# One common last slot behind the optional ones, its f32 mixing, and its columns cut as a half and two quarters

## The reference

```
x = x + mix(x, W0[c])                          # 64x64 per batch, across the rows, 16 choices
x = x + mix(x, W1[c])                          # the same c, so one 64x64 matrix does for both
x = x + x @ W2.T + 0.5 * (x @ A[l]) @ B.T      # shared 1024x1024 and a low-rank part, 5 choices
x = x + x @ W3[e].T                            # 1024x1024 per batch, e is one of 8, drawn from 3 to 7
```

## Time and profile before

| what | us |
|---|---|
| median of 3 runs (lowest, highest) | 395.53 (394.69, 395.9) |
| the profiled execution, its own time | 394.66 |
| its span in the profile | 392.9 |
| PE busy | 380.2 (97%) |
| DVE busy | 268.3 (68%) |
| ACT busy | 231.2 (59%) |
| POOL busy | 123.3 (31%) |
| end of the last DVE instruction | 388.18 |

### The profile page before, as it was taken

The page is one execution under the profiler, slowest core; times in us unless marked ns, Lnnn a source line. Parts: engine busy times, 40 slices in busy tenths (PEclk is TensorE's granted clock), DMA queues, the critical chain, the costliest instruction groups (busy, mean ns, idle before and its releaser), DMA issues.

```text
span 392.9 us, 7604 instructions
## 1 busy us (share of the span) xinstructions
PE 380.2 (97%) x1736; PEld 316.4 (81%) x1736; DVE 268.3 (68%) x285; ACT 231.2 (59%) x307; POOL 123.3 (31%) x163
## 2 busy tenths in 40 slices
PE   8999999999999999999999999899999999999990
PEld 8888888888888888888888887688888888888860
DVE  4746967865855958547967439953699546899563
ACT  3798859387232775244483549554677357777361
POOL 0000340100003000024865427763258434576400
PEclk9999999999999999999999999999999999999996
DMA  7984902740348475406526224742276322762223
GB/s 225 396 313 158 375 3 79 261 180 19 107 173 288 182 277 166 180 21 214 175 93 221 58 55 123 260 133 55 56 235 211 97 57 56 270 219 54 56 58 88
DMA packets 24219, 61.37 MB, mean 156 GB/s; under 512 B 1938, under 2 KB 2066, under 8 KB 24146
## 3 DMA queue, kind: packets, MB, share of 16 engines
q1 hardware_dynamic: 23808, 60.30, 46.1%
q10 hardware_dynamic: 338, 0.24, 0.2%
HBM read 52.15 MB, written 8.39 MB: 154 GB/s over the span
## 4 chain that ended last, share of the span: by engine, by line
PE 96%; issue 1%; DVE 1%; ACT 0%; POOL 0%; ACTq 0%; DVEq 0%; POOLq 0%
PE ps L1400 44%; PE ps L1286 13%; PE ps L1287 13%; PE ps L1288 13%; PE ps L1427 4%; PE ps L1313 4%; PE ps L1325 2%; PE ps L1257 1%; PE ps L1265 1%; DVE stage L1236 0%; DVE stage L1177 0%; ACT stage L706 0%; DVE aT L1214 0%; PE ps L1446 0%; ACT stage L798 0%
## 5 line engine op out<-in xcount | busy, mean ns | idle before, releaser
L1400 PE MATMUL ps<-ring,aT 128*128 x784 | 180.8, 389 | 0.0
L1400 PEld LDWEIGHTS ps<-ring,aT 128*128 128x128 f32 x784 | 147.1, 188 | 30.8 <-issue 0.4
L1286 PE MATMUL ps<-ring 128*128 128x512 f32 x224 | 88.3, 394 | 0.0
L1287 PE MATMUL ps<-ring 128*128 128x512 f32 x224 | 88.0, 393 | 0.0
L1288 PE MATMUL ps<-ring 128*128 128x512 f32 x224 | 87.9, 392 | 0.0
L429 POOL TENSOR_TENSOR aT<-xT,aT 128x512 fp32r<-128x512 f32 (+1 forms) x36 | 56.3, 1585 | 51.3 <-ACT aT L685 45.2
L1149 DVE TENSOR_TENSOR ring<-raw,ring 128x1024 f32 (+1 forms) x40 | 63.8, 1655 | 5.1 <-ACT ring L671 5.0
L694 ACT ACTIVATE aT<-ps 64x1024 fp32r<-64x1024 f32 x32 | 32.7, 1021 | 48.1 <-PE ps L1400 47.6
L1177 DVE TENSOR_TENSOR stage<-ps,stage 64x1024 f32<-64x1024 f32 x30 | 36.7, 1222 | 26.3 <-ACT stage L706 25.7
L1166 DVE TENSOR_TENSOR aT<-ps,aT 64x1024 fp32r<-64x1024 f32 x32 | 39.1, 1222 | 22.6 <-ACT aT L694 21.9
L1288 PEld LDWEIGHTS ps<-ring 128*128 128x128 f32 x224 | 42.6, 190 | 9.0
(11 more groups left out here) (82 smaller groups left out, 314.5 us busy)
## 6 DMA issues: line engine op xcount, KB each, us to landing
raw<-w3t SPq DMA_DIRECT2D x40, 512.0 KB, 4.4
ring_f<-xt SPq DMA_DIRECT2D x8, 1024.0 KB, 7.7
raw<-xt SPq DMA_DIRECT2D x8, 1024.0 KB, 5.1
out<-stage SPq DMA_DIRECT2D x30, 256.0 KB, 3.0
ring_f<-wt SPq DMA_DIRECT2D x4, 1024.0 KB, 7.4
xT<-xt SPq DMA_DIRECT2D x3, 1024.0 KB, 9.5
xT<-wt SPq DMA_DIRECT2D x2, 1024.0 KB, 15.2
ring_f<-xt SPq DMA_DIRECT2D x4, 256.0 KB, 6.4
```

What stands on the lines that cost most here:

```text
L1286: pe.matmul(dst, hi_of(qw)[:, k, cs], hi_of(qx)[:, k, :], start=start and k == 0, stop=False, skip_group_check=True)
L1287: pe.matmul(dst, hi_of(qw)[:, k, cs], lo_of(qx)[:, k, :], start=False, stop=False, skip_group_check=True)
L1400: last = pe.matmul(acc(i)[:, n, :], x3_split(i, k, start, P), ring[:, bass.ds(off + (part * D + n * 512), 512)], start=(k == 0 and j == 0) ...
```

## The change

The slots that may be missing now stand in front of one common last slot. With m = n_slots - 1, slots 0 to 14 run always, slots 15 to 18 stand nested in `If(n_slots > i + 1)`, and behind them comes the last slot, whose number m, plan word and semaphore counts are in registers. Since buffers alternate between odd and even slots, it is written twice, in `If(odd < 1)` and `Else`. Each engine reads the last slot's word and that of the slot ahead of it early, in slot 2 (`end_slot`; PE spreads its register work over slots 2, 3 and 4). All slots ahead of the last one have the regular order: 4 tiles, the mixing of slot i-1, 4 tiles.

In the last slot PE does the left 512 columns in 8 tiles, mixes the slot ahead, then does columns 512 to 767 in 8 tiles and columns 768 to 1023 in 6 and 2 tiles, with 256 columns to a matmul. Each part is mixed by a single f32 matmul with a matrix that POOL makes (`mixers_last`): ACT copies 128 rows of the sum to SBUF in f32 (`last_rows`), and no low part is split off. Both halves of the pair or both parts of the single sum are dealt with in this one matmul, so that one copy brings a part to `stage`: DVE copies the first two, ACT the third. Ahead of the last mixing stand 6 matmuls of 256 columns whose result isn't used (`warm(BRIDGE, ...)`). SP stores the first two parts, ACT the third. Stores count on two semaphores, for odd and even slots, in place of one for each slot, and SP waits for two semaphores at the end.

POOL also clears the 128x128 tile `last_mix` once, before slot 0. The core of the diff:

```diff
+LOOK = 2
...
-WARM = 20
+WARM, BRIDGE = 20, 6
...
-MIX_AT = 7
+END_AT = 6
...
+    last_mix = sb("last_mix", [P, P], F32, offset=cells_at)
+    last_row = sb("last_row", [P, D], F32, offset=aT_at + 4 * KT * CT)
...
-    def end_ps(i, h, n):
-        return acc(i - 1)[:, h, :] if n == 0 else mixed_ps[h][:, 1, :]
+    END_COLS = (slice(0, 512), slice(512, 768), slice(768, D))
+    def end_acc(p, part):
+        return (acc(p)[:, 0, :], acc(1 - p)[:, 1, 0:256], acc(p)[:, 1, 256:512])[part]
+    def end_ps(p, part):
+        return (acc(1 - p)[:, 0, :], acc(p)[:, 0, 0:256], acc(1 - p)[:, 1, 0:256])[part]
...
+    def end_slot(eng, n_slots):
+        more = eng.snap(n_slots & (SURE - 1))
+        m = within(eng, more + ENDS, ENDS, SLOTS - 1)
+        word, ahead = (eng.value_load(plan[0:1, bass.ds(m + at, 1)], min_val=0, max_val=2 ** WORD - 1) for at in (HEAD, HEAD - 1))
+        return m, within(eng, ((more + 1) >> 1) + ENDS // 2, ENDS // 2, (SLOTS - 1) // 2), word, ahead
+    def within(eng, value, lo, hi):
+        return nc.s_assert_within(eng.snap(value), lo, hi)
...
+            def last(p):
+                sp.wait_ge(s("end_sum"), 2)
+                store(1 - p, ahead, "end_ahead")
+                store_last(p, end_word)
+            with sp.If(odd < 1):
+                last(0)
+            with sp.Else():
+                last(1)
...
+            def mixers_last(word):
+                cs = [pool.value_load(toks[0:1, 0, bass.ds(b, 1)], min_val=0, max_val=NC_ - 1) for b in batches(word)]
+                def whole(rows, c, cols):
+                    one = as_f32(tab[rows, bass.ds(c, 1), :]).rearrange("p c n -> p (c n)")
+                    return pool.tensor_tensor(last_mix[rows, cols], one[:, 0:T], one[:, T:P], ALU.add)
+                with pool.If(get(word, SINGLE) < 1):
+                    whole(slice(0, P), cs[0], slice(0, T)).then_inc(s("end_st"), 1)
+                    pool.wait_ge(s("end_st"), 1)
+                    pool.memset(last_mix[T:P, 0:T], 0.0).then_inc(s("end_st"), 1)
+                    pool.wait_ge(s("end_st"), 2)
+                    whole(slice(T, P), cs[1], slice(T, P)).then_inc(s("end_st"), 1)
+                with pool.Else():
+                    whole(slice(0, P), cs[0], slice(0, T)).then_inc(s("end_st"), 3)
...
+            for i in range(ENDS):
                 earlier, word = step(i, earlier, word)
+                if i == LOOK:
+                    end_word = end_slot(pool, n_slots)[2]
             with contextlib.ExitStack() as nested:
-                for i in range(SURE, SLOTS):
-                    nested.enter_context(pool.If(n_slots > i))
+                for i in range(ENDS, SLOTS - 1):
+                    nested.enter_context(pool.If(n_slots > i + 1))
                     earlier, word = step(i, earlier, word)
+            mixers_last(end_word)
...
+            def last_rows(p, part):
+                act.wait_ge(s("end_left"), part + 1)
+                act.activation(last_row[:, END_COLS[part]], end_acc(p, part), ACT.Copy).then_inc(s("end_rows"), 1)
+            def last(p):
+                act.wait_ge(s("steps"), end_steps)
+                act.wait_ge(s("mixed"), end_mixed - 1)
+                rows_hi(1 - p)
+                act.wait_ge(s("mixed"), end_mixed)
+                last_rows(p, 0)
+                act.wait_ge(s(f"stored{1 - p}"), end_stored + 32 * (p - 1))
+                mixed_cols(1 - p, ahead)
+                last_rows(p, 1)
+                last_rows(p, 2)
+                act.wait_ge(s(f"stored{p}"), end_stored)
+                act.wait_ge(s("end_mixed"), 3)
+                act.activation(stage[:, p, END_COLS[2]], end_ps(p, 2), ACT.Copy).then_inc(s("end_out2"), 1)
+                act.wait_ge(s("end_out2"), 1)
+                act.dma_start(out_part(end_row, 2), stage[0:T, p, END_COLS[2]]).then_inc(s("end"), 16)
...
+            def last(p):
+                rows_lo(1 - p, two_ahead)
+                mixed_sum(1 - p, ahead, two_ahead, "end_sum")
+                dve.wait_ge(s(f"stored{p}"), end_stored)
+                for part in range(2):
+                    dve.wait_ge(s("end_mixed"), part + 1)
+                    dve.tensor_copy(stage[:, p, END_COLS[part]], end_ps(p, part)).then_inc(s("end_out"), 1)
...
+            def mix_last(p, part):
+                pe.wait_ge(s("end_st"), 3)
+                pe.wait_ge(s("end_rows"), part + 1)
+                pe.matmul(end_ps(p, part), last_mix[:, :], last_row[:, END_COLS[part]], start=True, stop=True)\
+                  .then_inc(s("end_mixed"), 1)
...
+                if i == LOOK:
+                    looked.extend(end_slot(pe, n_slots))
+                elif i == LOOK + 1:
+                    looked.append(record(looked[2]))
+                elif i == LOOK + 2:
+                    m = looked[0]
+                    looked.extend((pe.snap(m & 1), within(pe, m * 2, 2 * ENDS, 2 * SLOTS), within(pe, m * 4, 4 * ENDS, 4 * SLOTS)))
...
+            def end_products(p, passes, part, tiles=(0, KT)):
+                count8, offs, _ = end_record
+                cols = END_COLS[part]
+                for k in range(*tiles):
+                    if part == 0:
+                        pe.wait_ge(s("w_lo"), count8 + (k + 1 + WBASE - KT))
+                    off = offs[k // HALF] + (k % HALF) * UNIT
+                    for j, (start, split) in enumerate(passes):
+                        last = pe.matmul(end_acc(p, part), x3_split(p, k, start, P),
+                                         ring[:, bass.ds(off + (split * D + cols.start), cols.stop - cols.start)],
+                                         start=(k == 0 and j == 0), stop=(k == KT - 1 and j == len(passes) - 1))
+                if tiles[1] == KT:
+                    last.then_inc(s("end_left"), 1)
+            def last_slot(p):
+                def columns(passes):
+                    end_products(p, passes, 0)
+                    pe.wait_ge(s("st"), end_st)
+                    pe.wait_ge(s("r_lo"), end_r_lo)
+                    pe.wait_ge(s("staged"), end_r_lo - 2)
+                    mix(1 - p, get(ahead, SINGLE))
+                    end_products(p, passes, 1)
+                    mix_last(p, 0)
+                    end_products(p, passes, 2, (0, END_AT))
+                    mix_last(p, 1)
+                    end_products(p, passes, 2, (END_AT, KT))
+                pe.wait_ge(s("s_lo"), end_r_lo + 4)
+                pe.wait_ge(s("r_lo"), end_r_lo - 2)
+                with pe.If(end_record[2] < 1):
+                    columns(PAIR)
+                with pe.Else():
+                    columns(ALONE)
+                warm(BRIDGE, acc(1 - p)[:, 1, 256:512])
+                mix_last(p, 2)
...
+            ahead, end_record, odd, end_r_lo, end_st = looked[3:]
             with contextlib.ExitStack() as nested:
-                for i in range(SURE, SLOTS):
-                    with pe.If(n_slots == i):
-                        mix_last(i - 1, earlier[2], 1)
-                    nested.enter_context(pe.If(n_slots > i))
+                for i in range(ENDS, SLOTS - 1):
+                    nested.enter_context(pe.If(n_slots > i + 1))
                     earlier, mine = slot(i, earlier, mine)
-                mix_last(SLOTS - 1, earlier[2], 1)
+            with pe.If(odd < 1):
+                last_slot(0)
+            with pe.Else():
+                last_slot(1)
```

More of the change, by code:

```diff
@@ L464, in _ @@
             pool.wait_ge(s("plan"), 1)
+            pool.memset(last_mix[:, :], 0.0).then_inc(s("zeroed"), 1)
             adapter_eyes(0, 0)
@@ L472, in step @@
             def step(i, earlier, word):
[L473 to L478, removed]
+                following = slot_word(pool, i + 1)
+                slot_lo(i + 1, following)
                 if i == 0:
@@ L753, in step @@
                     adapter_part(i, word, LOAD_B, NEXT_B, (HALF, KT))
[L754 to L757, removed]
+                    act.wait_ge(s("mixed"), i)
+                    if i >= 3:
+                        act.wait_ge(*stored(i - 3))
+                    mixed_cols((i - 1) % 2, earlier)
                 return word, following
[L760 to L781, removed]
-                    second = slice(T // 2, T)
-                    for n in range(2):
-                        act.wait_ge(s("end_staged"), n + 1)
-                        act.dma_start(out_half(rows[0], n, second), stage[second, i % 2, 512 * n:512 * (n + 1)]).then_inc(s("end"), 16)
@@ L804, in _ @@
             with contextlib.ExitStack() as nested:
-                for i in range(SURE, SLOTS):
-                    with act.If(n_slots == i):
-                        last(i - 1, earlier)
-                    nested.enter_context(act.If(n_slots > i))
+                for i in range(ENDS, SLOTS - 1):
+                    nested.enter_context(act.If(n_slots > i + 1))
                     earlier, word = step(i, earlier, word)
-                last(SLOTS - 1, earlier)
+            with act.If(odd < 1):
```

(15 more changed lines are left out.)

253 lines of the change are left out of this document (94 added, 159 removed).

## The result

The changed kernel takes 398.44 us (six runs, 397.29 to 399.16) against 394.66 for the kernel before beside it: a ratio of 1.0091, with a 95% interval from 1.0072 to 1.011. It is slower by 0.9%, some 3.8 us. The profiled execution has a span of 397.2 us, 4.3 more than before. That lies in the wide range of the prediction, 391.8 to 401, and on the side it gave the largest chance, but 2.4 us from its point of 396.0 and outside the 394.6 to 397.5 that it gave the case it chose. The ratios leave out one run of the kernel before, beside e5 to e8, that took 777.88 us.

The account below looks back on a forecast made before the run. PE, busy 380.2 of 392.9 us, was taken as the bound. Tail -4.0, registers +0.3 and jumps +4.2 gave +0.5: span 393.4, median time 396.0 us; 8 in 10 range 391.8 to 401.

Parts of the forecast that it names:

- the case it chose: Two PE jumps before the last slot wait for code, clock stays up: 396.0 us, range 394.6 to 397.5, chance 0.38.
- third rival: Two PE jumps stop the array before the last slot and the clock falls: +4.5 us, 400.5, chance 0.30.
- The jumps: Before the last slot, PE waits for code at two jumps: stop of 3.7 to 5.1 us, M later by 4.2.
- The lead: At the end of slot 15, PE's sequencer reaches the jump 4.0 us ahead of the array.
- the lower of the two readings: PE's second jump waits for a fetch begun 0.7 us after resuming, ending 2.4 later: a stop of 3.7 us.
- The clock: Around the last slot, a fall to half clock after PE's stop, priced at +4.5 us, chance 0.30.
- Register work in slot 2: PE's early reads before slot 2's mixing take 2.0 us against 1.48 of waiting: +0.3 us (0 to 0.6).
- The tail: From M to the end of the span, 10.5 us instead of 14.5: -4.0 us (3.0 to 4.8).
- M: End of the mixing of slot 15, at 378.42 us in the kernel before; forecast to move by 4.2 us.
- the 0.17 for the low part: Before slot 15's mixing, PE's wait for the low part goes: 0.17 us off the stop at the jumps.

Follow-up runs that it names:

- e5: Changed kernel with every engine reading the last slot's words in slot 4 instead of slot 2: 399.13 us, ratio 1.011.
- e8: The kernel of e7 with every engine reading the last slot's words in slot 4: 391.85 us, ratio 0.9945.
- e1: Changed kernel with the single slot's arm written first in the last slot and the pair's in the Else: 395.34 us, ratio 1.0013.
- e2: Changed kernel without the code of slots 16 to 18 on all five engines: 392.63 us, ratio 0.9963.
- e3: Changed kernel without the code of slots 16 to 18 and with the single slot's arm first: 393.11 us, ratio 0.9958.
- e7: Changed kernel with PE's code alone reordered, copies of the last slot behind slot 15 and each later optional slot: 392.2 us, ratio 0.9943.
- e9: The kernel of e7 with PE's early register work alone moved to slots 4 and 5: 391.35 us, ratio 0.9921.
- e6: Kernel before without the code of slots 17 to 19 on all five engines: 393.03 us, ratio 0.9961.
- e4: Changed kernel with three idle f32 matmuls of 512 columns on PE between the two jumps: 396.43 us, ratio 1.006.

## Why the prediction was right, and where it was off

The range held, and slower was the likeliest side. But the case that the prediction chose, two jumps with the clock up, isn't the one that came. What came is its third rival, two jumps with the clock down, and that was put at 400.5. That the time lies in the range rests in part on luck: it lies between a forecast without the fall of the clock and a rival that priced the fall at 4.5 us, twice what it cost.

*The jumps.* The place and the two branches were as forecast, and e1, e2, e3 and e7 show each of them by taking it away. That they wait for code is read from the q8 fetches inside them. The stop was 5.0 us, inside the 3.7 to 5.1 given. The steps beneath it were off. The lead was 374.2 - 370.9 = 3.3 us and not 4.0. I had read it at the branch that ends slot 14's products, and the condition comes 0.2 us behind that branch; the rest is that the sequencer was 3.5 us ahead at the branch itself, for which I have no cause. The first jump took 4.24 us and not 4.0. The second took 2.9 us, and ended 2.4 us after its fetch began: that is the lower of the two readings, only with a fetch that began 1.1 us after the first jump and not 0.7.

*The clock.* I had made its fall a rival of 0.30 and left it out of the point. It fell, inside the stop of 5.0 us, and this is the step that failed: the size of the forecast lacks this term. The row that bore on it, an idle stretch of 3.4 us with the clock down behind it, was read right, and should have weighed more for a stop that I myself put at 3.7 or more. The price was 2.2 us, a little under the least of my 2.4 to 10 and half of the 4.5 that the rival took: the clock came back after 4 us of products.

*Register work in slot 2.* 0.9 us instead of 0.3. PE's reads and what goes with them took 2.7 us, from 212.3 to 215.0, and not 2.0. The two reads themselves, shortest, middle and longest in ns:

```profile
L266 PEldq TENSOR_LOAD <-plan x2: 315/601/887, 212.7 to 213.5; - x2
```

The first took the 0.31 that I had used for both, the second 0.89. In the kernel before a read on PE had taken 0.87 too, at 374.0, which the earlier trace rows leave out. With 2.7 in the place of 2.0, 1.2 us stick out of the wait of 1.48 instead of 0.5, and the queue hid 0.3 of them. e9 shows that the wait can be taken away.

*The tail.* -3.3 instead of -4.0. The f32 mixing took 0.86 and 0.43 us as taken, the quarters 1.91 for 16. DVE's and SP's path was the later one, and SP issued its last store 7.4 us after M, both as forecast. But that store landed 3.3 us after its issue began, and not 2.5. It has 64 rows of 1 KB, where I had used a store of 32 rows of 2 KB, but that isn't shown to be the reason: the same store landed after 2.2 us in e1 and 2.8 in e3. What differs is how long its issue takes on SP: 1.32 us here, begun 0.3 us after ACT's last issue began, and 0.58 in e1 and 0.47 in e3, where it didn't come so close behind ACT's. That the two issues get into each other's way is a reading of these rows; no run isolates it.

*What the tail is worth.* Of the 3.3 us, much is not the shorter chain. e6 has 390.6 - 378.3 = 12.3 us from the end of that mixing to the end of its span, so about 2.1 come from SP's jump and the waits behind it (1.6 by the medians of e6 and the kernel before), and some 1.2 to 1.7 from the f32 mixing and the quarters.

Together: +0.5 was forecast, +4.3 came. The difference of 3.8 is the clock (2.2), the stop (5.0 and not 4.4, which is the 4.2 of the sum with the 0.17 for the low part put back: 0.6), slot 2 and the slots after it (1.0) and the tail (0.7), less 0.5 in the first stage and 0.3 more than forecast in the mixing of slot 15. These make 3.7, and the last 0.1 is rounding. The first stage ends between 185.8 and 187.2 in the twelve traces, so its 0.5 is within what executions differ by.

## What to carry to other kernels

Code that is skipped isn't free on the engine that sets the time: here a jump over an arm of 82 matmuls cost 1.8 to 2.9 us and one over three slots 4.0 to 4.3, where skipping a slot's arm of 24 cost 0.34 at most. It is hidden only by what the sequencer is ahead, 3.3 us here. So lay the likeliest path out straight, and put a rare case in the far `Else`. Two jumps in a row add up, since there is no time to get ahead again between them. Put register work where the sequencer was waiting anyway, for each engine by its own waits.

## What was not expected of the hardware

- A jump over three slots' code took 4.0 to 4.3 us on PE wherever it stood, and one over only the unused copy of the last slot nearly as much (3.8 to 4.2 in the changed kernel and e1 to e4, behind the last mixing). One over the pair's arm took 1.8 to 2.9. The shorter times are those in which a q8 fetch had begun ahead of the branch: at 370.2 for the branch at 370.9 in e2 (1.8 us), at 369.7 for the one at 370.2 in e7 (2.2 us). Right behind the long jump it began 0.4 us after the branch, and that took 2.9 us.
- A stop of 5.0 us let the clock fall to 1.2 GHz inside it, and it was back at 2.4 GHz after 4 us of 512-column products. A stop of 2.2 us left it full in the one execution of e1 with a trace, and so did the waits of 1.3 to 1.5 us in slot 5 of each kernel where I looked.
- A read of a plan word on PE took 0.31 us or 0.89 us, one right behind the other in slot 2.
- A store of 64 KB in rows of 1 KB landed 2.2 to 3.3 us after its issue began, and its issue alone took 0.47 to 1.38 us on SP.
